# Two attention layers and an MLP for 16 sequences on one core: attention values four units behind their batch, VectorE's unit step reordered, first weight chunks split on two engines

## What is computed

```python
# layer 0: LayerNorm with conditioned scale and shift, 16 heads of 32, keys and values from a latent of 128
q = (h @ Wq.T); c_kv = h @ Wkd.T; k = c_kv @ Wku.T; v = c_kv @ Wvu.T   # 4 key heads
scores = where(mask, -inf, rotary(q) @ rotary(k).T / sqrt(32))   # block, window, every 64th key
x = x + (softmax(scores) @ v) @ Wo.T
# layer 1: conditioned RMS norm, 8 heads of 64, one key head, no mask
x = x + (softmax(rotary(q) @ rotary(k).T / 8) @ v) @ Wo.T
h = ada_rms(x)
out = x + (silu(h @ Wg.T) * (h @ Wu.T)) @ Wd.T                   # 512 -> 2048 -> 512
```

## Time and profile before

| | |
|---|---|
| median of three runs | 2262.89 us (2262.89 to 2264.32) |
| the profiled execution: its own time | 2270.03 us |
| the profiled execution: span of the core | 2268.1 us |
| PE busy, share of the span | 1804.4 us, 80% |
| DVE busy | 1121.4 us, 49% |
| ACT busy | 935.5 us, 41% |
| POOL busy | 739.2 us, 33% |
| mean granted clock of PE | 0.896 |
| start of rounds 0 to 7 (first product of the latent) | 24, 251, 530, 800, 1070, 1339, 1609, 1879 us |
| start of the last MLP | 2149 us |

### The profile page before, as it was taken

One profiled execution on the slowest core, in us unless ns is written; L12 is line 12 of the kernel. 1 busy time (PEld: TensorE's weight loads), 2 busy tenths in 40 slices (PEclk: granted clock), 3 DMA queues, 4 the chain that ended last, 5 costly groups with the idle time before them and its releaser, 6 DMA issues.

```text
span 2268.1 us, 34380 instructions
## 1 busy us (share of the span) xinstructions
PE 1804.4 (80%) x10072; PEld 896.3 (40%) x10072; DVE 1121.4 (49%) x3050; ACT 935.5 (41%) x2769; POOL 739.2 (33%) x876
## 2 busy tenths in 40 slices
PE   6563977879778897878978698687977879787899
PEld 2232533435334443444434353343533444344444
DVE  6664544635547354454555445463554735546321
ACT  4533444434544335334453345443454434533320
POOL 3785576231333214232131412323133221323120
PEclk9686987989989898989989799898998989898999
DMA  8653567333553245442553325533355324644220
GB/s 232 132 122 67 151 149 173 88 65 95 127 121 70 58 124 133 91 80 76 116 129 90 74 77 132 121 87 63 92 130 116 76 57 119 130 99 80 75 93 19
DMA packets 527217, 234.05 MB, mean 103 GB/s; under 512 B 476336, under 2 KB 493744, under 8 KB 527024
## 3 DMA queue, kind: packets, MB, share of 16 engines
q1 hardware_dynamic: 511472, 175.09, 36.4%
q10 hardware_dynamic: 15552, 56.63, 8.2%
HBM read 90.09 MB, written 16.78 MB: 47 GB/s over the span
## 4 chain that ended last, share of the span: by engine, by line
PE 60%; DMA 10%; DVE 9%; POOL 7%; issue 7%; ACT 5%; SPq 1%; DVEq 0%; POOLq 0%; ACTq 0%
PE gate L1451 6%; PE gate L1452 6%; PE gate L1453 6%; PE up L1451 6%; PE y L1555 6%; PE up L1452 6%; PE up L1453 5%; DMA prob_t<-prob 5%; DMA stack<-prob 4%; POOL prob L727 3%; PE bank L1451 3%; PE bank L1452 3%; PE bank L1453 3%; DVE work L1153 3%; PE y L1451 2%
## 5 line engine op out<-in xcount | busy, mean ns | idle before, releaser
L727 POOL TENSOR_TENSOR prob<-work,prob 128x512 f16<-128x512 f32 (+1 forms) x320 | 339.2, 1063 | 859.9 <-ACT prob L898 859.9
L898 ACT ACTIVATE prob<-work 128x512 f16<-128x512 f32 (+1 forms) x320 | 188.7, 590 | 555.6 <-DVE work L1153 554.4
L889 ACT ACTIVATE bank<-bank,low 128x128 f32<-128x128 f32 (+2 forms) x768 | 298.5, 390 | 26.8 <-DVE low L1130 16.7
L720 POOL TENSOR_TENSOR inner_t<-inner,inner_t 128x512 f16<-128x512 f32 x128 | 148.9, 1163 | 360.5 <-ACT inner_t L1070 360.3
L1406 DVE SCALAR_TENSOR_TENSOR silu<-silu,gate 128x512 f32<-128x512 f32 x128 | 87.8, 686 | 295.7 <-ACT silu L1064 295.7
L1451 PE MATMUL up<-mlp,ring 128*128 128x512 f16 x512 | 205.2, 401 | 19.3 <-DVE inner L1416 19.3
L1451 PE MATMUL gate<-mlp,ring 128*128 128x512 f16 x512 | 208.4, 407 | 15.1 <-POOL ring L785 8.3
L1555 PE MATMUL y<-prob_t,v_hi 128*64 128x256 f16 (+3 forms) x640 | 108.7, 380 | 129.7 <-DMA stack<-prob 94.7
L1452 PE MATMUL gate<-mlp,ring 128*128 128x512 f16 x512 | 207.2, 405 | 0.0
L1453 PE MATMUL gate<-mlp,ring 128*128 128x512 f16 x512 | 206.0, 402 | 0.0
L1452 PE MATMUL up<-mlp,ring 128*128 128x512 f16 x512 | 204.7, 400 | 0.0
(11 more groups left out here) (174 smaller groups left out, 3915.8 us busy)
## 6 DMA issues: line engine op xcount, KB each, us to landing
ring<-wgu_dram ACTq DMA_DIRECT2D x108, 512.0 KB, 3.6
x_in<-x_dram SPq DMA_DIRECT2D x18, 512.0 KB, 3.4
x_res<-x_mid SPq DMA_DIRECT2D x16, 512.0 KB, 3.1
wgu_dram<-ring SPq DMA_DIRECT2D x16, 512.0 KB, 3.4
out_dram<-x_res SPq DMA_DIRECT2D x32, 256.0 KB, 2.3
inner_t<-wd_t_dram SPq DMA_DIRECT2D x4, 1024.0 KB, 7.2
ring<-wg_t_dram SPq DMA_DIRECT2D x16, 256.0 KB, 3.9
ring<-wu_t_dram SPq DMA_DIRECT2D x16, 256.0 KB, 4.3
```

What stands on the lines that cost most here:

```text
L720: pool.tensor_tensor(inner_t[:, 1, f, :], inner[:], inner_t[:, 0, f, :], ALU.subtract).then_inc(inner_low, 1)
L727: pool.tensor_tensor(terms(prob[:, g % SLOTS, 1, :], layer, j), terms(scaled_prob[g % SLOTS], layer, j), terms(prob[:, g % SLOTS, 0, :], l ...
L889: ins = act.activation(bank_[:, at:at + wid], bank_[:, at:at + wid], ACT.Exp, bias=low[:, j % BANKS, k:k + 1], scale=-1.0, accum_out=total)
L898: act.activation(terms(prob[:, g % SLOTS, 0, :], layer, j), terms(scaled_prob[g % SLOTS], layer, j), ACT.Copy).then_inc(hi_done, 1)
```

## The change

1. LAG becomes 4: the values of batch b are done behind the scores of unit 4b+9, and heads follow two steps later. The heads of tile 1 of both sequences (before: of the second alone) now fall into `finish`, where PE does the two projections of tile 0, the last values, then the two projections of tile 1. SLOTS, OWN and TURNED keep their numbers.
2. VectorE's unit step becomes: reciprocal and scaling of unit j, then the gates and inners, then the minima of unit j+2.
3. PLAN is dealt anew. Parts ahead of layer 0's units: 26 before, 17 after; in its units 39 and 36; between them and layer 1's units 8 and 10; in these 16 and 23; in the finish and the fill of the MLP's input 5 and 8; at the end 2 and 2. From query0 to query1 of layer 0 they were six and are three.
4. Of a chunk POOL makes only the two highs, with the scale folded in; VectorE makes the two lows, with one operation each, after the gates of the chunk before.
5. The big splits come in another order and at other steps: wq1 and wo1 alternate through layer 0's units, wd0 stays ahead of the root of layer 0's finish (where wd1 and wd0 stood), wd3 comes behind that root, wd1 behind the root of layer 1's finish, and wd2 in four pieces in the first steps of round 1. Loads move with them.
6. The angles move from unit 6 of layer 1 to `out1b.1`, behind POOL's last low of the layer and ahead of the root; the first two chunks of round 0 to `out1a.0`. The LayerNorm statistics of the next pair come four units later.
7. Round 1 is written out ahead of VectorE's loop.

The core of the diff (the rest of PLAN, of which the first line stands here, is item 3):

```diff
-AHEAD, LAG = 2, 2
+AHEAD, LAG = 2, 4
...
-                + [(f"heads{layer}", 1, 1)]
+                + [(f"heads{layer}", s, 1) for s in BOTH]
...
-PLAN = [("fill0.0", 0), ("fill0.1", 4), ("lat.0", 3), ("lat.1", 1), ("kv.0", 2), ("kv.1", 1),
...
+PLAN = [("fill0.0", 0), ("fill0.1", 2), ("lat.0", 2), ("lat.1", 1), ("kv.0", 2), ("kv.1", 1),
...
-LN_STATS, LN_APPLY = {"unit1_3": 0, "unit1_5": 1}, {"unit1_7": 0, "unit1_9": 1}
+LN_STATS, LN_APPLY = {"unit1_7": 0, "unit1_9": 1}, {"unit1_11": 0, "unit1_13": 1}
...
-SPLIT_AT = {f"unit0_{3 + 2 * c}": [("wq1", c)] for c in range(CH)}
-SPLIT_AT |= {f"unit0_{13 + 2 * c}": [("wo1", c)] for c in range(CH)}
+BIG = ["wq1", "wo1", "wd0", "wd3", "wd1", "wd2"]
+SPLIT_AT = {f"unit0_{3 + 5 * c}": [("wq1", c)] for c in range(CH)}
+SPLIT_AT |= {f"unit0_{5 + 5 * c}": [("wo1", c)] for c in range(CH)}
 SPLIT_AT |= {step: [(key, c) for c in range(CH)] for step, key in (
-    ("out0a.0", "wd1"), ("out0b.0", "wd0"), ("kv1.0", "wd2"), ("kv1.1", "wd3"))}
+    ("out0b.0", "wd0"), ("fill2.0", "wd3"), ("fill4.0", "wd1"))}
+SPLIT_LATER_AT = {step: [("wd2", c)] for c, step in enumerate(
+    ("kv.0", "query0.0", "query1.0", "stack0.0"))}
+BIG_ORDER = [key_c for dealt in (SPLIT_AT, SPLIT_LATER_AT) for step, _ in PLAN
+             for key_c in dealt.get(step, ())]
 EARLY = 2
-FIRST_CHUNKS_AT = "unit1_6"
+FIRST_CHUNKS_AT = "out1a.0"
...
-LOADS_AT = {"lat.0": ["wkv1"], "kv.0": ["wo1"], "unit0_12": ["wd1"], "unit0_19": ["wd0"],
-            "unit0_22": ["wd2"], "out0a.0": ["wd3"]}
+LOADS_AT = {"lat.0": ["wkv1"], "kv.0": ["wo1"], "unit0_19": ["wd0"], "unit0_22": ["wd3"],
+            "unit0_23": ["wd1"], "fill2.0": ["wd2"]}
 RAW_AT = {"fill2.0": 0, "kv1.0": 1}
 
 
-ANGLES_AT, SINES_AT = "unit1_6", "end"
+ANGLES_AT, SINES_AT = "out1b.1", "end"
...
+                    if step in ("fill2.0", "fill4.0"):
+                        for s in BOTH:
+                            root(n, ("fill2.0", "fill4.0").index(step), s)
                     if m is None:
                         for key, c in SPLIT_AT.get(step, ()):
                             big_split_(key, c)
                         if step == FIRST_CHUNKS_AT:
                             for f in range(EARLY):
-                                chunk_scale(f)
-                                chunk_halves(f)
-                    if step in ("fill2.0", "fill4.0"):
-                        for s in BOTH:
-                            root(n, ("fill2.0", "fill4.0").index(step), s)
+                                chunk_highs(f)
...
+                        for key, c in SPLIT_LATER_AT.get(step, ()):
+                            big_split_(key, c)
                         for f in chunks_at(m, step, 4):
-                            if f + 2 < FCH:
-                                chunk_halves(f + 2)
+                            if f + EARLY < FCH:
+                                chunk_highs(f + EARLY)
                             inner_lows(m, [f])
-                            if f + 3 < FCH:
-                                chunk_scale(f + 3)
...
-            def chunk_scale(f):
+            def chunk_highs(f):
                 pool.wait_ge(chunk_in[f % 2], 32 * (f // 2 + 1))
-                for m in range(2):
-                    pool.tensor_scalar(raw_chunk(f)[:, m], raw_chunk(f)[:, m], WS, 1.0, ALU.mult,
-                                       ALU.mult).then_inc(chunk_scaled, 1)
-
-            def chunk_halves(f):
-                pool.wait_ge(chunk_scaled, 2 * f + 2)
                 if f < EARLY:
                     pool.wait_ge(cond_used, 4 * CH)
                 else:
-                    pool.wait_ge(u_full, f - 2 + 1)
+                    pool.wait_ge(u_full, f - EARLY + 1)
                     pool.wait_ge(chunk_out[f % 2], 16 * (f // 2))
-                hi, lo = (ring[:, f % 2, :, half].rearrange("p m c n -> p m (c n)")
-                          for half in range(2))
                 for m in range(2):
-                    pool.tensor_scalar(hi[:, m], raw_chunk(f)[:, m], 1.0, 1.0, ALU.mult,
-                                       ALU.mult).then_inc(chunk_high, 1)
-                for m in range(2):
-                    pool.wait_ge(chunk_high, 2 * f + m + 1)
-                    ins = pool.tensor_tensor(lo[:, m], raw_chunk(f)[:, m], hi[:, m], ALU.subtract)
-                ins.then_inc(chunk_split, 1)
+                    pool.tensor_scalar(ring[:, f % 2, m, 0].rearrange("p c n -> p (c n)"),
+                                       raw_chunk(f)[:, m], WS, 1.0, ALU.mult, ALU.mult).then_inc(
+                                           chunk_high, 1)
...
+                heads(n, layer, 0, 1)
...
                                 gates(m, [f])
+                                if at_start(m) and EARLY <= f + 1 < FCH:
+                                    chunk_lows(f + 1)
...
                     step = f"unit{layer}_{j}"
+                    inverses(n, layer, j)
+                    scale_probs(n, layer, j)
                     between(m, step)
+                    if j + 2 < total:
+                        lows(n, layer, j + 2)
                     if step in LN_STATS:
                         ln_stats((n[0], n[1] + 1), LN_STATS[step])
                     elif step in LN_APPLY:
                         ln_apply((n[0], n[1] + 1), LN_APPLY[step])
-                    inverses(n, layer, j)
-                    if j + 2 < total:
-                        lows(n, layer, j + 2)
-                    scale_probs(n, layer, j)
...
-                for s in BOTH:
-                    add(n, layer, s, 0)
+                add(n, layer, 0, 0)
+                heads_low(n, layer, 0, 1)
+                add(n, layer, 1, 0)
                 between(m, f"heads{layer}.0", f"heads{layer}.1")
-                add(n, layer, 0, 1)
                 heads_low(n, layer, 1, 1)
                 between(m, f"out{layer}b.0", f"out{layer}b.1")
-                add(n, layer, 1, 1)
+                for s in BOTH:
+                    add(n, layer, s, 1)
...
+                if m is None:
+                    for f in range(EARLY):
+                        chunk_lows(f)
+
+            def chunk_lows(f):
+                for m in range(2):
+                    dve.wait_ge(chunk_high, 2 * f + m + 1)
+                    hi, lo = (ring[:, f % 2, m, half].rearrange("p c n -> p (c n)")
+                              for half in range(2))
+                    ins = dve.scalar_tensor_tensor(lo, raw_chunk(f)[:, m], WS, hi, ALU.mult,
+                                                   ALU.subtract)
+                ins.then_inc(chunk_split, 1)
...
                 for s in BOTH:
                     between(m, f"out{layer}a.{s}")
                     project(n, layer, s, 0, w)
-                for s in BOTH:
-                    between(m, f"heads{layer}.{s}")
-                project(n, layer, 0, 1, w)
+                between(m, f"heads{layer}.0")
                 batch_values(n, layer, UNITS[layer] // BATCH - 1)
+                between(m, f"heads{layer}.1")
                 for s in BOTH:
                     between(m, f"out{layer}b.{s}")
-                project(n, layer, 1, 1, w)
+                    project(n, layer, s, 1, w)
...
                 t, j = divmod(part - 4 * FCH, 8)
+                if part == 4 * FCH and first:
+                    split_wait(pe, "wd2")
```

More of the change, by code:

```diff
@@ L370, in build @@
         big_high, big_scaled, big_split = sem("big_high"), sem("big_scaled"), sem("big_split")
[L371 to L372 removed]
+        chunk_high, chunk_split = sem("chunk_high"), sem("chunk_split")
         chunk_in, chunk_out = sems("chunk_in"), sems("chunk_out")
@@ L733, in layers @@
                 tables(n)
-                if first:
-                    chunk_scale(EARLY)
                 for step, _ in PLAN:
@@ L1068, in inner_highs @@
                 for f in chunks:
+                    if at_start(n) and f in (0, FCH // 2):
+                        split_wait(act, ("wd3", "wd2")[f // (FCH // 2)])
                     need(act, inner_ready, count(n, FCH, f + 1))
@@ L1439, in _ @@
             layer1((None, 0), None)
-            with dve.Fori(0, NP - 1) as i:
-                layer0((i, 1), (i, 0))
-                layer1((i, 1), (i, 0))
+            layer0((None, 1), (None, 0))
+            layer1((None, 1), (None, 0))
+            with dve.Fori(0, NP - 2) as i:
+                layer0((i, 2), (i, 1))
+                layer1((i, 2), (i, 1))
             for f in range(FCH):
@@ L1660, in mlp_part @@
             def mlp_part(n, part):
+                first = at_start(n)
                 if part < 4 * FCH:
@@ L1666, in mlp_part @@
                         need(pe, low_made, count(n, LOW_USES, LOW_USES))
-                    first = n[0] is None and n[1] == 0
                     place = f % 2 if first else f % RING
@@ L1706, in _ @@
                            "out0a.0": ["wo0"], "kv1.0": ["wkv1"], "query2.0": ["wq1"],
-                           "out1a.0": ["wo1"], "end": ["wd3"]}
```

(1 more changed line is left out.)

9 lines of the change are left out of this document (3 added, 6 removed), and 30 rows, old and new, of the table PLAN.

## The result

The changed kernel takes **1825.48 us** (median of four runs, 1824.03 to 1828.57) against 2262.89 us: a ratio of 0.807, 95% interval 0.8056 to 0.8084. The profiled execution has a span of 1823.7 us.

The account below looks back on a forecast made before the run. PE sets the pace, losing time to waits for transposed terms and a lower clock. Six loop rounds −258, round 1 −46, round 0 −28: −332 on 2270.0 us, median 7.1 lower, so 1931 us; range 1845 to 2060.

Parts of the forecast that it names:

- Both together cover nearly all of the 39.3 us: −39: Loop round: values two steps later and scaling ahead of the minima remove PE's waits for transposed terms, −39 us.
- the half microsecond for the scaling: Unit chain: scaling ahead of the minima takes 0.5 us out, more where gates or inners stood ahead.
- The last batch of a layer (+5): Loop round: each layer's last batch lacks six steps behind it, 2.5 us of wait per layer, +5 us (0 to 10).
- VectorE's and ScalarE's waits (+4): Layer 0's units: both engines have less time per unit; half a microsecond in each of eight units, +4 us (0 to 8).
- query1 (+2): Layer 0: fewer MLP parts cover query1's wait for VectorE's rotation of query0, +2 us (0 to 3.8).
- The clock, −15: Loop round: work PE lost at the lower clock comes back, −15 us, with ends of 4 and 23.7.
- Rival D: Loop round: all slow-clock time was lost work, 23.7 us instead of 15, 1868 us in all; chance 0.08.
- rival B: Layer 0's units: ScalarE becomes the pace, a loop round gives −34, 2000 us in all; chance 0.18.
- Round 1: Round 1: the loop's −43, −8 for POOL's weight lows, +5 for VectorE's lows and wd2's split: −46 us (−20 to −56).
- Round 0: Round 0, without MLP: −17 for the block moved and −11 for later values: −28 us (−15 to −50).
- the block (−17): Round 0: first chunks and angles, holding POOL 17.2 us between two layer-1 lows, go behind the units, −17 us.
- rival A: Layer 1: unraised places for transposed terms keep its 18 us of waits, 2110 us in all; chance 0.11.

Follow-up runs that it names:

- e2: Kernel before with only VectorE's new unit-step order (scaling ahead of gates, inners and minima): 2106.66 us, ratio 0.9291.
- e14: Kernel before with only the minima moved behind the scaling in VectorE's unit step: 2134.79 us, ratio 0.9428.
- e1: Kernel before with only LAG 4 and the finish that goes with it: 1963.12 us, ratio 0.8658.
- e3: Changed kernel with LAG 2 and the finish of before, all else as changed: 2010.66 us, ratio 0.8867.
- e9: Kernel before with LAG 4, its finish and VectorE's new unit step, nothing else: 1883.14 us, ratio 0.8319.
- e12: Changed kernel with the block of first chunks' highs and angles at unit 6 of layer 1 again: 1833.26 us, ratio 0.8103.
- e11: Changed kernel, but in round 1 POOL makes chunk highs ahead of the step's probability low and wd2's piece: 1818.82 us, ratio 0.8036.

## Why the prediction was wrong

The loop round was to lose 43 us and lost 61.2. Six times these 18.2 us are 109 of the 112 us by which the spans' difference (444 us) exceeds the forecast's 332; round 0 gave 10 us more than forecast, round 1 gave 5 less.

- *"Both together cover nearly all of the 39.3 us: −39"* was right: 39.3 to 1.7 us. The working under it was not. The lag alone left 10 us, and the half microsecond for the scaling was read from one unit in which neither gates stood ahead nor the minima had to wait. The order saves about 2 us in each chain (e2), mostly at the minima, which held it for 1.0 us in layer 0 and 1.8 in layer 1 (e14).
- *The terms added back, +2, +5 and +4,* are the step that failed. The last batch of a layer (+5) waits for nothing: the only value wait of the round is in batch 1 of layer 0. It had not waited in the kernel before either: the eight waits there are those of other batches, and the last of layer 0 starts right behind a projection (first two lines below the list). VectorE's and ScalarE's waits (+4) did not grow: inner and silu end 2.6 us of PE's waits now and 3.7 before. query1 (+2) waits 1.3 instead of 0.7 us. And two kinds of wait that had no term went too. One is ahead of the last projection of a layer (act_lo, 3.0), where VectorE's low of the heads was awaited: another projection now stands between the last values and that one (e1), or in e3, with the finish of before, a part. The other is for score banks (2.0), gone in e2 too, so by the earlier scaling. In place of +11 these waits gave −5.6: with 37.6 of waits for values and 18.5 of clock they make 61.7, half a microsecond over the round's 61.2.
- *The clock, −15,* measured 18.5: PE's busy time for the same matmuls, 220.6 to 202.1 us. The mechanism was right and the size short by 3.5. Rival D, all of the slow time as lost work, had 23.7 and is 5.2 off the other way. The Trainium skill's rule ("TensorE: Matmul & The Clock Gate", section Terms) is that of rival D, and the trace has less than it gives, 18.5 us.
- *ScalarE as the pace (rival B)* did not come. Layer 0's units last 62 us, with ACT busy for 50.7: 82%, about the load that was worked out (47.6 in 56 us, 85%). The load was real, and PE's waits behind it stayed at the 2.6 us above.
- *Round 1,* −46, measured −41. The wait for POOL's lows went, as forecast, and a wait for VectorE's came in its place, 12.2 us for 8.3. The low was priced at 0.68 us and takes 1.18 (last section). The view of the earlier trace rows has the same form for another weight, wo, at 0.95 (last line below the list): the row taken was the cheaper one.
- *Round 0,* −28, measured −37.6. "PE waits for the chain whatever the lag" was the error: the lag alone shortens the round by 20.1 us, the order alone by 13.0 and both by 22.7 (e9), where −11 stood for later values. Behind them the other items take the remaining 14.9, the block (−17) among them. Its share is open: the shortened one is worth 5 us (e12).

The start of the last batch of layer 0 in the kernel before, without idle time behind a projection, and VectorE's low of wo there:

```profile
946.74 0.38 PE L1453 MATMUL bank<-wo_hi,act_lo 128*128 128x512 f16 x1
947.05 0.28 PE L1555 MATMUL y<-stack,v_hi 128*32 128x256 f16 x1
...
L1400 DVE SCALAR_TENSOR_TENSOR wo_lo<-inner_t,wo_hi 128x512 f16<-128x512 f32 x4 | 3.8, 952 | 0.1
```

As the prediction asked, waits below 8 us, the clock of the loop above 0.97 and no wait for POOL's lows are all there; its sign for rival A, layer 1 waiting while layer 0 doesn't, is absent.

## What to carry to other kernels

Where in-order engines pass units along a chain, put the step that releases the chain ahead of any step that waits for the next unit: the price of the wrong order is that step's wait, not only its duration. Before crediting a wait that stands first in line, ask what the engine would wait for next (27 us at the gates became 24 at the minima). And when the consumer is made later by enough steps, credit the waits behind it and the time that PE's own work lost at the lower clock (18.5 us of a round here), and add a leftover only where the kernel before has a wait at that place, rather than one for each engine that only gets busier.

## What was not expected of the hardware

The low of a chunk on VectorE took 1.18 us on average in round 1, where the same form took 0.68 for wq before; in e11 it took 1.04:

```profile
L1369 DVE SCALAR_TENSOR_TENSOR ring<-ring 128x512 f16<-128x512 f32 x28 | 31.9, 1178 | 3.3 <-POOL ring L773 3.0
...
L1370 DVE SCALAR_TENSOR_TENSOR ring<-ring 128x512 f16<-128x512 f32 x28 | 28.0, 1039 | 0.0
```

In the timeline of e11, two of them take 2.64 us beside POOL's work, and POOL's next operation took 1.58 us, where its kind took 1.16 on average in the loop before. Two others, beside which POOL did nothing, in the same round of the changed kernel:

```profile
214.78 1.28 DVE L1369 SCALAR_TENSOR_TENSOR ring<-ring 128x512 f16<-128x512 f32 x2
```

The five lows of that round beside which POOL did nothing took 0.68 to 0.69 us each; of the 23 with an operation of POOL beside them, 20 took 0.86 to 1.66. The Trainium skill ("GPSIMD Engine Reference", Specifications) says that POOL shares its SBUF interfaces with VectorE, with contention when a VectorE instruction has two SBUF inputs; the lows have two, and the trace agrees in the durations on both engines.

The transposes got slower as the kernel got faster. In the layer-0 units the DMA engines' share rose from 0.60 to 0.98, and a transpose into prob_t took 4.4 us (median) from issue to landing instead of 3.1. The transposes of these units before, then after:

```profile
stack<-prob SPq DMA_TRANSPOSE x12, 4.1
prob_t<-prob SPq DMA_TRANSPOSE x10, 3.1
...
stack<-prob SPq DMA_TRANSPOSE x12, 4.8
prob_t<-prob SPq DMA_TRANSPOSE x11, 4.4
```

Only one batch waits for a transpose now. It is what a still faster layer 0 would meet next; that was argued from this share and not tried.
